# A gated cross-attention and channel-mix block: softmax denominators summed on ScalarE, queries stacked through DRAM, values loaded in two parts

## The chip, the cores and the metric

One core of one Trainium2 chip runs the whole program. The metric is device time in microseconds; three runs of the kernel before give a median of 3099.62 (3092.7 to 3100.64).

## What is computed

64 independent batches of 256 tokens with 512 features; 16 heads of 32 features. Cut to what matters, all in fp32:

```python
q = layernorm(x)                                   # [64, 256, 512]
qs, ks, vs = relu(heads(q)), relu(heads(ctx)), relu(heads(ctx))
att = softmax(einsum('bthf,byhf->bhty', qs, ks) / sqrt(32))
o = einsum('bhty,byhf->bhtf', att, vs)
x = x + tanh(g_xattn) * relu(o @ ffn_w.T + ffn_b)
n = layernorm(x); n_prev = n shifted by one token
xr, xk = mu_r * n + (1 - mu_r) * n_prev, mu_k * n + (1 - mu_k) * n_prev
x = x + tanh(g_ffn) * sigmoid(xr @ W_r) * (square(relu(xk @ W_k)) @ W_v)
```

## The kernel before

Matmul operands that need more precision than the fast matmul type gives are split into a high and a low part. A dense product is three matmuls (high x high, low x high, high x low; `product`, L944). For the scores, 96 rows hold the pieces instead: q as high, high, low and k as high, low, high, over 32 features each.

The work is a software pipeline over batches. An iteration `i` holds the attention of batch i, the projection and mixing of batch i - 1, the channel mix of batch i - 2 and the last sums of batch i - 3. The loop body is written twice, for the two values of `par`. Each engine has its own list of calls in `iteration`; those lists, written by hand, set the order of work. An engine executes its list strictly in order and waits on semaphores. On TensorE (the list from L1005) an iteration has 16 **slots**. Slot k begins with `shifted_scores(i, k)` (L911) and holds two dense parts (`dense`), six matmuls of 256 or three of 512 columns each, and the scores of the head seven further on.

The steps of attention in that order:

- `scores` (L899) computes query by key scores of one head into one of two PSUM banks, `s_bank`. `head_max` (L693, VectorE) takes each row's negative maximum, from which `turn_m` (L877), `copy_m` (L702) and the DMA `move_m` (L277) make row 96 of `q_st`. `scores` waits for `s_maxed` of the head two before.
- `shifted_scores` (L911) computes key by query scores with the maximum subtracted; `exponent` (L492, ScalarE) makes `probs` from them. The factor 1/sqrt(32) is the exponent's `scale`.
- `values` (L925) multiplies four heads' `probs` with `v_pos`. `denominators` (L937) multiplies the same `probs` with ones. `norm_o` (L712, L714, VectorE) takes the reciprocal of 128x256 denominators and multiplies.
- `write_o`, `read_o` (SP) carry the result through DRAM into `o_mv`. `o_high` (L499, ScalarE) and `o_low` (L362, GpSimd) split it, and `project` uses it.
- For q, `norm_1` (L663, VectorE) normalizes `x_ln`; `q_high` (L465, L466, ScalarE, two copies) and `q_low` (L669, VectorE) make `q_nat`. Eight `turn_q` (L868) per batch turn it, and eight `q_stack` (L473, ScalarE) copy it to `q_st`.
- `load_x1` (L451) and `load_v` (L457) are DMAs in ScalarE's queue. `load_x1` waits for the store of an earlier batch. `relu_v` (L684) is VectorE's.

All turns (of q, maxima and normalized x1) share one PSUM bank, `tp_bank`, and each waits for the copy that empties it:

```python
users = [copy_of(*t) for t in reversed(turns[:n])]
users += [copy_of(t[0], t[1] - 1, *t[2:]) for t in reversed(turns)]
```

Of the kernel before, what the change touches and what calls it, by code (L numbers as in the profile page):

```python
# [16 lines left out]
def flamingo_block(nc, x, ctx_in, ctx_t, g_xattn, g_ffn, w_t, bias, mu, out):  # L17
# [24 lines left out]
    SCALE = float(HD) ** -0.5  # L42
# [5 lines left out]
    with es:  # L48
# [10 lines left out]

        k_dram = nc.dram_tensor("k_dram", [2, CH, 2, HD, GR, T], F32, kind="Internal").ap()  # L60

# [4 lines left out]
        q_nat = sb("q_nat", [P, NU, HEADS, 3, HD], F32R)  # L66
# [6 lines left out]
        o_val = sb("o_val", [P, T])  # L73
        o_mv = sb("o_mv", [P, 2 * GR, T // GR])
# [45 lines left out]
        v_loaded = sem("v_loaded")  # L120
# [19 lines left out]
        q_stacked = sem("q_stacked")  # L140
# [11 lines left out]
        pv_ready = sem("pv_ready")  # L152
        rden_ready = sem("rden_ready")
        o_ready = sem("o_ready")
# [32 lines left out]
        out_ready = sem("out_ready")  # L187

# [30 lines left out]
        def _(sp):  # L219
# [13 lines left out]
            def load_x(b):  # L233
                if on(b):

                    after(sp, q_lo_ready, 2 * b)
                    after(sp, q_hi_ready, 2 * b)

# [32 lines left out]

            def move_m(b, c):
# [22 lines left out]

            def store(b, par):
                if on(b):
                    sp.wait_ge(out_ready, NU * (b + 1))
                    sp.dma_start(out[b].rearrange("(u p) d -> p u d", p=P), x1[:, par, :, :]).then_inc(stored, 16)

            def iteration(i, par):
                stack_k(i, 3, par)
                store(i - 3, 1 - par)
# [12 lines left out]
                stack_k(i + 1, 2, 1 - par)  # L316
                move_m(i + 1, 0)
                load_w(i)
                read_o(i, 0)
                write_o(i, 2)  # L320
# [13 lines left out]
        def _(pool):  # L334
# [15 lines left out]
            def rstd_2(b, u):  # L350
                if on(b):
# [3 lines left out]
                                            ALU.pow).then_inc(rstd2_ready, 1)  # L355

# [50 lines left out]
            def iteration(i, par):  # L407
                rstd_1(i + 1)
                ka_square(i - 2, 0)
                ka_square(i - 2, 1)  # L410
                o_low(i - 1, 1)
# [8 lines left out]
                xk_low(i - 1, 1)  # L420
                o_low(i, 0)
# [5 lines left out]
        def _(act):  # L427
# [25 lines left out]
            def load_v(b):  # L453
                if on(b):

                    after(act, pv_ready, CH * b)
                    act.dma_start(v_pos[:, :, :], ctx_in[b].rearrange("(v p) d -> p v d", p=P)).then_inc(v_loaded, 16)  # L457

            def q_high(b, u):
                if on(b):  # L460
                    act.wait_ge(x_normed, NU * b + u + 1)

                    after(act, q_turned, 2 * CH * b)
# [720 lines left out]
```

## Time and profile before

| what | value |
|---|---|
| median of three runs | 3099.62 us |
| the profiled execution | 3097.49 us, its span 3095.6 us |
| instructions | 70938 |
| TensorE's mean granted clock | 0.988 |
| DMA | 408.56 MB, mean 132 GB/s |

The page gives busy time by engine. Matmuls are pipelined, so TensorE's busy share says that something was in the array, not that it streamed at its peak. The chain of waits follows the last instruction back through whatever released each step, and "issue" in it is time for which the profile shows no cause. `PEld` is TensorE's weight load, `SPq` and `ACTq` are the sequencers of SyncE and ScalarE at work on DMAs.

### The profile page before, as it was taken

How to read it: one execution, taken by the hardware profiler on the slowest of the kernel's cores; microseconds unless marked ns; L12 is line 12 of the kernel's file. 1: busy time of each engine (PE TensorE's matmuls, PEld its weight loads, DVE VectorE, ACT ScalarE, POOL GpSimd, SP SyncE). 2: the span in 40 equal slices, each digit the busy share in tenths (PEclk: the TensorE clock that was granted, in tenths of full speed). 3: DMA queues.
4: the chain of work that ended last, by engine and by line, in shares of the span. 5: the costliest groups of instructions: out<-in, count | busy, mean ns of one | idle time of the engine just before them, and what ended most of it. 6: DMA issues, size and time to landing. Idle time of an engine off the chain costs nothing.

```text
span 3095.6 us, 70938 instructions
## 1 busy us (share of the span) xinstructions
PE 2882.7 (93%) x23168; PEld 2202.3 (71%) x23168; DVE 2326.9 (75%) x4111; ACT 1568.8 (51%) x2828; POOL 1049.3 (34%) x902
## 2 busy tenths in 40 slices
PE   3899999999999999999999999999999999999998
PEld 2677777777777777777777777777777777777776
DVE  5777777777777777777877777777777777778774
ACT  3445455455554555454555555554554545555542
POOL 0233333333332333333333333333333333333333
PEclk9999999999999999999999999999999999999999
DMA  4544435535435445445445354454454444454431
GB/s 163 147 125 132 143 110 149 149 108 151 140 115 149 135 124 146 127 131 144 125 135 147 107 150 137 118 152 129 125 149 127 131 143 125 140 146 130 132 107 40
DMA packets 387850, 408.56 MB, mean 132 GB/s; under 512 B 163553, under 2 KB 295649, under 8 KB 387810
## 3 DMA queue, kind: packets, MB, share of 16 engines
q1 hardware_dynamic: 352994, 340.92, 38.6%
q10 hardware_dynamic: 34816, 67.12, 6.7%
q8 instruction: 24, 0.39, 0.1%
q14 instruction: 16, 0.13, 0.0%
HBM read 272.64 MB, written 134.22 MB: 131 GB/s over the span
## 4 chain that ended last, share of the span: by engine, by line
PE 57%; DVE 15%; DMA 9%; issue 8%; SPq 7%; ACT 1%; ACTq 1%; DVEq 0%; POOL 0%; POOLq 0%
PE bank L944 28%; DMA out_dram<-x 8%; PE bank L925 7%; PE bank L911 6%; PE bank L899 5%; PE bank L937 4%; DVE m_nat L693 4%; DVE o_val L712 4%; SPq L270 3%; DVE st L647 2%; DVE k_raw L677 2%; PE bank L886 2%; PE bank L868 2%; SPq L256 2%; SPq L268 2%
## 5 line engine op out<-in xcount | busy, mean ns | idle before, releaser
L492 ACT ACTIVATE probs<-bank 128x512 f32<-128x512 f32 x1024 | 596.3, 593 | 481.4 <-PE bank L911 260.4
L693 DVE TENSOR_REDUCE m_nat<-bank 128x2 fp32r<-128x512 f32 x1024 | 688.4, 683 | 79.4 <-PE bank L899 78.7
L473 ACT ACTIVATE q_st<-bank 96x512 fp32r<-96x512 f32 x512 | 304.5, 595 | 717.2 <-PE bank L868 717.0
L911 PE MATMUL bank<-q_st,k_st 97*128 97x256 f32 x2048 | 451.3, 302 | 61.0 <-ACT probs L492 43.0
L712 DVE RECIPROCAL o_val<-bank 128x256 f32<-128x256 f32 x256 | 449.1, 1754 | 62.3 <-PE bank L937 54.5
L911 PEld LDWEIGHTS bank<-q_st,k_st 97*128 97x128 f32 x2048 | 341.7, 191 | 154.1 <-issue 56.4
L899 PE MATMUL bank<-k_st,q_st 96*128 96x256 f32 x2048 | 431.3, 293 | 7.6 <-DMA k_st<-k_dram 5.0
L899 PEld LDWEIGHTS bank<-k_st,q_st 96*128 96x128 f32 x2048 | 357.9, 192 | 59.6 <-issue 6.4
L395 POOL TENSOR_TENSOR xm<-xm 128x512 f32<-128x512 f32 x128 | 133.6, 1043 | 782.6 <-ACT xm L536 782.6
L925 PE MATMUL bank<-probs,v_pos 128*32 128x256 f32 x4096 | 282.0, 393 | 99.3 <-issue 98.6
L362 POOL TENSOR_TENSOR o_lo<-o_mv,o_hi 128x512 fp32r<-128x512 f32 x128 | 164.3, 1284 | 524.9 <-ACT o_hi L499 524.9
L702 DVE CAST m_t<-bank 4x256 fp32r<-4x256 f32 x256 | 105.0, 410 | 270.5 <-PE bank L877 270.4
L944 PE MATMUL bank<-xk_hi,w_hi 128*128 128x256 f32 x1024 | 298.4, 291 | 0.0
L944 PE MATMUL bank<-xk_lo,w_hi 128*128 128x256 f32 x1024 | 286.5, 280 | 0.0
L944 PE MATMUL bank<-xk_hi,w_lo 128*128 128x256 f32 x1024 | 286.3, 280 | 0.0
L937 PE MATMUL bank<-probs,ones_r 128*32 128x256 f32 x4096 | 284.4, 397 | 0.0
L925 PEld LDWEIGHTS bank<-probs,v_pos 128*32 128x32 f32 x4096 | 113.5, 110 | 222.6 <-issue 150.4
L868 PEld LDWEIGHTS bank<-ident_r,q_nat 128*96 128x96 f32 x2048 | 193.6, 127 | 71.3 <-issue 52.4
L868 PE MATMUL bank<-ident_r,q_nat 128*96 128x128 f32 x2048 | 219.7, 231 | 24.1 <-DVE q_nat L669 20.5
L380 POOL TENSOR_TENSOR xk_lo<-xm,xk_hi 128x512 fp32r<-128x512 f32 x128 | 164.4, 1285 | 215.1 <-ACT xk_hi L523 183.4
L354 POOL TENSOR_TENSOR rstd<-ve,mhalf 128x1 f32<-128x1 f32 x128 | 69.3, 542 | 446.2 <-DVE ve L730 446.2
L944 PE MATMUL bank<-w_hi,o_hi 128*128 128x512 f32 x512 | 209.4, 409 | 4.2 <-POOL o_lo L362 4.2
(90 smaller groups left out, 6128.1 us busy)
## 6 DMA issues: line engine op xcount, KB each, us to landing
k_st<-k_dram SPq DMA_DIRECT2D x256, 256.0 KB, 3.7
k_raw<-ctx_t_dram SPq DMA_DIRECT2D x256, 128.0 KB, 4.2
x_ln<-x_dram SPq DMA_DIRECT2D x256, 128.0 KB
k_dram<-k_high SPq DMA_DIRECT2D x64, 512.0 KB, 3.0
k_dram<-k_raw SPq DMA_DIRECT2D x64, 512.0 KB, 4.5
k_st<-k_dram SPq DMA_DIRECT2D x256, 128.0 KB, 3.6
v_pos<-ctx_dram ACTq DMA_DIRECT2D x64, 512.0 KB, 5.8
o_dram<-o_val SPq DMA_DIRECT2D x256, 128.0 KB, 1.7
```

Source lines behind the costliest of these rows:

```text
L362: nc.gpsimd.tensor_tensor(by_tile(o_lo, u), o_mv[:, :, :].rearrange("p g (k a) -> p k g a", k=KC), by_tile(o_hi, u).bitcast(F32), ALU.subt ...
L380: nc.gpsimd.tensor_tensor(xk_lo[:, part, :], xm[:, part, :], xk_hi[:, part, :].bitcast(F32), ALU.subtract).then_inc(xk_lo_ready, 1)
L473: nc.scalar.activation(q_st[0:QK, c, :, P * u:P * u + P], tp_bank[0:QK, :].rearrange("p (g t) -> p g t", g=GR), ACT.Copy).then_inc(q_stack ...
L492: nc.scalar.activation(probs[:, n // GR % 2, n % GR, :, :].rearrange("p v t -> p (v t)"), st_bank[n % 2][:, :], ACT.Exp, scale=SCALE).then ...
L693: nc.vector.tensor_reduce(m_nat[:, c % 2, :, n % GR:n % GR + 1], s_bank[n % 2][:, :].rearrange("p (u y) -> p u y", u=NU), AX_X, ALU.max, n ...
L712: nc.vector.reciprocal(o_val[:, :], pv_bank[:, T:2 * T]).then_inc(rden_ready, 1)
L868: mm = nc.tensor.transpose(tp_bank[0:QK, P * g:P * g + P].bitcast(F32R), q_nat[:, u, GR * c + g, :, :], ident_r[:, :])
L899: mm = nc.tensor.matmul(s_bank[n % 2][:, T * u:T * u + T], q_st[0:QK, c, g, P * u:P * u + P], k_st[0:QK, c, g, :], start=True, stop=True)
L911: mm = nc.tensor.matmul(st_bank[n % 2][:, T * v:T * v + T], k_st[0:ST, c, g, P * v:P * v + P], q_st[0:ST, c, g, :], start=True, stop=True)
L925: nc.tensor.matmul(pv_bank[HD * g:HD * g + HD, 0:T], v_pos[:, v, HD * h:HD * h + HD], probs[:, c % 2, g, v, :], start=(v == 0), stop=(v == ...
L937: mm = nc.tensor.matmul(pv_bank[HD * g:HD * g + HD, T:2 * T], ones_r[:, 0:HD].bitcast(F32), moving, start=(n == 0), stop=(n == len(sums) - 1))
L944: mm = nc.tensor.matmul(dst, lhs[a], rhs[c], start=first and n == 0, stop=last and n == 2)
```

## The change

- **Denominators.** `denominators` is gone. `sum_exp(b, n, par)` on ScalarE takes the exponents of one head's query by key scores in place in `s_bank`, with the head's negative maximum as bias, in two instructions of 128x256 (one per half of the queries); the accumulator output writes the sum to `den`. `scores` now waits for `s_summed` of the head two before. Per batch VectorE takes one reciprocal of 128x32 (`recip`), TensorE turns it (`turn_rden`), VectorE copies it (`copy_rden`). SP writes it to DRAM (`write_rden`) and reads it back in four DMAs, broadcast over 32 partitions (`read_rden`). GpSimd multiplies `o_mv` by it in place (`o_scale`), before `o_high`. `norm_o` becomes a plain copy (`copy_o`).
- **Scale.** The 1/sqrt(32) moves into the layer norm's variance, which is multiplied by 32, so that the maximum and both scores carry it.
- **Queries.** `norm_1` writes the normalized x with its features in another order to `q_low_t`. Two `turn_q` per batch turn it in fp32, four 128x128 transposes each. `q_high` takes one relu out of PSUM, `q_low` the rest. `write_q` and `stack_q` carry both parts through `q_dram` into `q_st`, in four and eight DMAs per batch. `q_stack` is gone.
- **Values.** Columns 0 to 383 of batch i + 1 are loaded in iteration i, behind `exponent(i, 14)`; columns 384 to 511 of batch i in iteration i. `relu_v` follows in two parts.
- **Order.** `norm_1` stands right behind `head_max(i, 7)`, and `load_x1` behind `exponent(i, 3)`.

```diff
+            def write_q(b, par):
+                if on(b):
+                    sp.wait_ge(q_hi_ready, NU * (b + 1))
+                    sp.wait_ge(q_lo_ready, NU * (b + 1))
+                    for u in range(NU):
+                        for half, tile in enumerate((x_ln[:, u, :].rearrange("p (c t) -> p c t", c=CH),
+                                                     q_low_t[:, u, :, :])):
+                            sp.dma_start(q_dram[par, :, half].rearrange("c f g t -> (f g) c t")[:, :, P * u:P * u + P],
+                                         tile).then_inc(q_written, 16)
+            def stack_q(b, c, par):
+                if on(b):
+                    sp.dma_start(q_st[0:HD, c, :, :].bitcast(F32), q_dram[par, c, 0]).then_inc(q_stacked[c], 16)
+                    sp.dma_start(q_st[HD:QK, c, :, :].bitcast(F32),
+                                 q_dram[par, c].rearrange("h f g t -> (h f) g t")).then_inc(q_stacked[c], 16)
...
+            def read_rden(b):
+                if on(b):
+                    sp.wait_ge(rden_written, 16 * (b + 1))
+                    for m in range(GR):
+                        sp.dma_start(rd_mv[HD * m:HD * m + HD, :, :],
+                                     rden_dram.rearrange("h (m r) -> m h r", m=GR)[m:m + 1].broadcast_to([HD, HEADS, T // GR])
+                                     ).then_inc(rd_moved, 16)
...
             def iteration(i, par):
                 stack_k(i, 3, par)
+                stack_q(i, 3, par)
                 store(i - 3, 1 - par)
...
                 stack_k(i + 1, 0, 1 - par)
+                write_q(i + 1, 1 - par)
                 move_m(i, 2)
+                queries_written(i + 1)
+                stack_q(i + 1, 0, 1 - par)
                 write_o(i, 0)
                 stack_k(i + 1, 1, 1 - par)
+                stack_q(i + 1, 1, 1 - par)
                 load_x(i + 2)
...
+            def o_scale(b, u):
+                if on(b):
+                    pool.wait_ge(rd_moved, 16 * GR * (b + 1))
+                    pool.wait_ge(o_moved, 16 * GR * (NU * b + u + 1))
+                    nc.gpsimd.tensor_tensor(o_mv[:, :, :], o_mv[:, :, :], rd_mv[:, 2 * GR * u:2 * GR * u + 2 * GR, :],
+                                            ALU.mult).then_inc(o_scaled, 1)
...
             def q_high(b, u):
                 if on(b):
+                    act.wait_ge(q_turned, NU * b + u + 1)
+                    nc.scalar.activation(x_ln[:, u, :].bitcast(F32R), tp_bank[:, :], ACT.Relu).then_inc(q_hi_ready, 1)
...
+            def sum_exp(b, n, par):
+                if on(b):
+                    act.wait_ge(s_maxed, HEADS * b + n + 1)
+                    for u in range(NU):
+                        scores = s_bank[n % 2][:, T * u:T * u + T]
+                        last = nc.scalar.activation(scores, scores, ACT.Exp,
+                                                    bias=m_nat[:, n // GR % 2, u, n % GR:n % GR + 1].bitcast(F32),
+                                                    accum_out=den[:, par, n, u:u + 1])
+                    last.then_inc(s_summed, 1)
...
             def scores(b, n):
...
-                        pe.wait_ge(q_stacked, 2 * CH * b + 2 * c + 2)
+                        pe.wait_ge(q_stacked[c], 32 * (b + 1))
                         pe.wait_ge(k_stacked[c], 32 * (b + 1))
-                    after(pe, s_maxed, HEADS * b + n - 1)
+                    after(pe, s_summed, HEADS * b + n - 1)
...
-                turns = [("q", i, 2, 1), ("m", i, 1, 0), ("q", i, 3, 0), ("q", i, 3, 1),
-                         ("m", i, 2, 0), ("q", i + 1, 0, 0), ("q", i + 1, 0, 1), ("q", i + 1, 1, 0),
-                         ("x", i - 1, 0, 0), ("m", i, 3, 0), ("x", i - 1, 0, 1), ("q", i + 1, 1, 1),
-                         ("m", i + 1, 0, 0), ("q", i + 1, 2, 0)]
+                turns = [("m", i, 1), ("q", i + 1, 0), ("q", i + 1, 1), ("m", i, 2),
+                         ("x", i - 1, 0), ("m", i, 3), ("x", i - 1, 1), ("rden", i, 0), ("m", i + 1, 0)]
```

Three places in the order of instructions matter below. First ScalarE around the exponent of slot 2 (`probs<-bank`). Before, from the load of x1 in front of it to the load of the values:

```order
L192 ISA
L451 ISA [waits stored]
L451 DMA x<-x_dram 128x2x512
L485 REGISTER_ALU
L492 ACTIVATE probs<-bank 128x512 [waits st_ready]
L533 ISA
L535 REGISTER_ALU [waits kt_ready]
L536 ACTIVATE xm<-bank 128x512 [waits xk_lo_ready]
L470 REGISTER_ALU
L473 ACTIVATE q_st<-bank 96x4x128 [waits st_ready,q_turned]
L457 ISA [waits pv_ready]
L457 DMA v_pos<-ctx_dram 128x2x512
```

After, from the same exponent to the values' load (L555 is `sum_exp`, L529 `q_high`, L601 `kt_relu`):

```order
L546 ACTIVATE probs<-bank 128x512 [waits st_ready]
L552 REGISTER_ALU
L555 ACTIVATE bank,den<-bank,m_nat 128x256 [waits s_maxed]
L555 ACTIVATE bank,den<-bank,m_nat 128x256
L528 ISA
L529 ACTIVATE x_ln<-bank 128x512 [waits q_turned]
L598 ISA
L600 REGISTER_ALU [waits kt_ready]
L601 ACTIVATE xm<-bank 128x512 [waits xk_lo_ready]
L208 ISA
L522 ISA [waits pv_ready]
L522 DMA v_pos<-ctx_dram 128x2x128
```

The load of x1 has left this place, the values' load is a quarter of its size, and the relu of q comes behind two summing exponents.

Second, TensorE at the second turn of q, at the end of slot 2, in the kernel after:

```order
L1030 MATMUL bank<-xk_hi,w_lo 128x256
L1030 MATMUL bank<-xk_lo,w_hi 128x256
L1030 MATMUL bank<-xk_hi,w_hi 128x256
L1030 MATMUL bank<-xk_hi,w_lo 128x256
L1030 MATMUL bank<-xk_lo,w_hi 128x256
L955 REGISTER_ALU
L958 MATMUL bank<-ident_r,q_low_t 128x128 [waits q_lo_ready,x_normed]
L958 MATMUL bank<-ident_r,q_low_t 128x128 x3
L208 REGISTER_ALU
L1009 MATMUL bank<-q_st,k_st 128x256 [waits exp_ready]
```

The four transposes wait for `q_lo_ready`, the low half of the first turn; the next shifted scores stand behind them.

Third, GpSimd at the start of an iteration. Before:

```order
L395 TENSOR_TENSOR xm<-xm 128x512 [waits kt_relued]
L393 REGISTER_ALU
L395 TENSOR_TENSOR xm<-xm 128x512 [waits kt_relued]
L359 ISA
L362 TENSOR_TENSOR o_lo<-o_mv,o_hi 128x4x128 [waits z_ready,o_hi_ready]
L388 TENSOR_TENSOR xr_lo<-xd,xr_hi 128x1024 [waits r_ready,xr_hi_ready,xr_ready]
```

After:

```order
L458 TENSOR_TENSOR xm<-xm 128x512 [waits kt_relued]
L456 REGISTER_ALU
L458 TENSOR_TENSOR xm<-xm 128x512 [waits kt_relued]
L415 ISA
L416 ISA [waits rd_moved]
L417 TENSOR_TENSOR o_mv<-o_mv,rd_mv 128x512 [waits o_moved]
L425 TENSOR_TENSOR o_lo<-o_mv,o_hi 128x4x128 [waits z_ready,o_hi_ready]
```

The scaling of `o_mv` stands between the second squaring (of what `kt_relu` gives) and the low part of o.

## Rows read from the trace of the kernel before

**Rows 1.** The page, part 1: busy us, share of the span, instructions.
```profile
PE 2882.7 (93%) x23168; PEld 2202.3 (71%) x23168; DVE 2326.9 (75%) x4111; ACT 1568.8 (51%) x2828; POOL 1049.3 (34%) x902
```

**Rows 2.** The chain that ended last, 1500 to 1600 us: start, length, what.
```profile
1503.72 0.38 ACTq L451
...
1509.52 1.17 issue
...
1517.79 0.24 PE bank L911 x2
1518.03 0.70 PE bank L944 x3
...
1524.55 1.00 PE bank L937 x16
1525.55 0.59 PE bank L886 x4
...
1528.94 0.25 PE bank L868 x4
...
1549.93 0.39 ACTq L451
...
1555.70 2.75 issue
...
1599.08 0.39 ACTq L451
```

**Rows 3.** Waits, whole run: who for whom: us in total, times, longest.
```profile
ACT probs L492 <- DMA out_dram<-x: 210.9, 60, 5.1
...
DVE v_pos L684 <- DMA v_pos<-ctx_dram: 133.5, 61, 3.3
...
PE bank L911 <- ACT probs L492: 43.0, 60, 2.3
```

**Rows 4.** Windows: stretch, length, busy by engine, TensorE's granted clock, DMA share, GB/s.
```profile
1551.00:1558.50 7.50, 4.67 (x25) 3.44 (x29) 2.14 (x4) 4.82 (x11) 2.08 (x2) 1.00 1.00 262
1558.50:1564.00 5.50, 5.50 (x46) 3.46 (x47) 3.64 (x5) 3.33 (x6) 3.90 (x2) 0.69 0.23 48
```

**Rows 5.** Timeline of ScalarE: start, length, instruction.
```profile
1552.92 1.08 ACT L492 ACTIVATE probs<-bank 128x512 f32<-128x512 f32 x2
```

**Rows 6.** Groups by form, 1500 to 1788 us, ScalarE: busy us, mean ns | idle before.
```profile
L492 ACT ACTIVATE probs<-bank 128x512 f32<-128x512 f32 x97 | 56.5, 593 | 48.3 <-DMA out_dram<-x 24.2 <-PE bank L911 23.2
...
L481 ACT ACTIVATE k_high<-k_raw 128x1024 fp32r<-128x1024 f32 x6 | 6.3, 1048 | 0.0
```

**Rows 7.** Timeline of VectorE around the start of an iteration.
```profile
1542.48 0.68 DVE L763 SCALAR_TENSOR_TENSOR th<-th,bank 128x512 f32<-128x512 f32 x1
1543.19 0.75 DVE L766 SCALAR_TENSOR_TENSOR x<-th,tgh,x 128x512 f32<-128x512 f32 x1
1543.86 0.41 DVE L702 CAST m_t<-bank 4x256 fp32r<-4x256 f32 x1
1544.47 1.76 DVE L712 RECIPROCAL o_val<-bank 128x256 f32<-128x256 f32 x1 [0.20 <-PE bank L937]
...
1546.60 1.66 DVE L755 SCALAR_TENSOR_TENSOR xd<-xd,mu_sb,xt 128x256 f32<-128x256 f32 x4
1548.18 0.68 DVE L693 TENSOR_REDUCE m_nat<-bank 128x2 fp32r<-128x512 f32 x1
1548.79 0.99 DVE L663 TENSOR_SCALAR x_ln<-x_ln,mv,rstd 128x512 f32<-128x512 f32 x2
1549.69 1.28 DVE L693 TENSOR_REDUCE m_nat<-bank 128x2 fp32r<-128x512 f32 x2
```

**Rows 8.** Groups by form, 1500 to 1788 us, GpSimd.
```profile
L362 POOL TENSOR_TENSOR o_lo<-o_mv,o_hi 128x512 fp32r<-128x512 f32 x12 | 15.4, 1283 | 44.6 <-ACT o_hi L499 44.6
L395 POOL TENSOR_TENSOR xm<-xm 128x512 f32<-128x512 f32 x12 | 12.5, 1042 | 74.6 <-ACT xm L536 74.6
```

**Rows 9.** The page, part 2: what the DMA moved.
```profile
DMA packets 387850, 408.56 MB, mean 132 GB/s; under 512 B 163553, under 2 KB 295649, under 8 KB 387810
```

More of the change, by code:

```diff
@@ L139, in flamingo_block @@
         q_turned = sem("q_turned")
-        q_stacked = sem("q_stacked")
+        q_written = sem("q_written")
+        q_stacked = [sem(f"q_stacked{c}") for c in range(CH)]
         v_ready = sem("v_ready")
@@ L410, in iteration @@
                 ka_square(i - 2, 1)
+                o_scale(i - 1, 1)
                 o_low(i - 1, 1)
@@ L420, in iteration @@
                 xk_low(i - 1, 1)
+                o_scale(i, 0)
                 o_low(i, 0)
@@ L924, in values @@
                             h = GR * c + g
-                            nc.tensor.matmul(pv_bank[HD * g:HD * g + HD, 0:T], v_pos[:, v, HD * h:HD * h + HD],
-                                             probs[:, c % 2, g, v, :], start=(v == 0), stop=(v == NU - 1))
-            def denominators(b, c):
-                if on(b):
-                    after(pe, o_ready, CH * b + c)
-                    sums = [[probs[:, c % 2, g, v, :] for g in range(GR)] for v in range(NU)]
-                    for n, per_head in enumerate(sums):
-                        for g, moving in enumerate(per_head):
-                            mm = nc.tensor.matmul(pv_bank[HD * g:HD * g + HD, T:2 * T], ones_r[:, 0:HD].bitcast(F32),
-                                                  moving, start=(n == 0), stop=(n == len(sums) - 1))
+                            mm = nc.tensor.matmul(pv_bank[HD * g:HD * g + HD, 0:T], v_pos[:, v, HD * h:HD * h + HD],
+                                                  probs[:, c % 2, g, v, :], start=(v == 0), stop=(v == NU - 1))
                     mm.then_inc(pv_ready, 1)
@@ L1052, in iteration @@
                 values(i - 1, 3)
-                turn(1)
-                denominators(i - 1, 3)
+                turn(0)
                 dense(0, 2)
@@ L1057, in iteration @@
                 dense(0, 3)
-                turn(2)
+                turn(1)
                 shifted_scores(i, 2)
@@ L1080, in iteration @@
                 values(i, 0)
-                turn(4)
-                denominators(i, 0)
+                turn(3)
                 shifted_scores(i, 6)
-                turn(5)
                 dense(3, 0)
@@ L1092, in iteration @@
                 scores(i, 14)
-                turn(6)
                 dense(3, 3)
@@ L1098, in iteration @@
                 scores(i, 15)
-                turn(7)
                 dense(4, 1)
@@ L1104, in iteration @@
                 values(i, 1)
-                turn(8)
+                turn(4)
                 scores(i + 1, 0)
                 dense(4, 3)
-                turn(9)
+                turn(5)
                 shifted_scores(i, 10)
                 dense(5, 0)
-                denominators(i, 1)
-                turn(10)
+                turn(6)
                 scores(i + 1, 1)
@@ L1120, in iteration @@
                 dense(5, 3)
-                turn(11)
+                turn(7)
                 shifted_scores(i, 12)
@@ L1130, in iteration @@
                 values(i, 2)
-                turn(12)
+                turn(8)
                 scores(i + 1, 4)
@@ L1137, in iteration @@
                 scores(i + 1, 5)
-                denominators(i, 2)
-                turn(13)
                 dense(7, 1)
```

189 lines of the change are left out of this document (115 added, 74 removed).

## The prediction

> **What bounds the kernel now.** The busy line comes first: TensorE is busy 93% of the span, VectorE 75%, ScalarE 51% [rows 1]. So TensorE sets the pace, and the questions are how much matmul time an iteration holds and what makes TensorE wait. The profiled execution took 3097.5 us (span 3095.6), 0.07% under the median of 3099.6. A difference under about 0.3% could not be told from no change here.
>
> The chain of waits gives the period. Its load of x1 comes at 1503.72, 1549.93 and 1599.08 us [rows 2], so two iterations take 95.36 us, and one 47.68. The same rows show two kinds of loss: "issue" stalls of 1.17 and 2.75 us in front of the matmuls with the values. The waits by pair tell why [rows 3]. VectorE waits 133.5 us in 61 times for the values' DMA. That DMA stands in ScalarE's queue behind the load of x1, which waits for the store of an earlier batch (210.9 us in 60 times). TensorE's next shifted scores then wait for the late exponent, 43.0 us in 60 times, 0.7 each. In the stretch before the 2.75 us stall the DMA engines are full (share 1.00, 262 GB/s), and behind it TensorE's granted clock is 0.69 for 5.5 us, a mix of its two levels, 1.2 and 2.4 GHz [rows 4]. The shorter stall of the neighbouring iteration leaves no such mark.
>
> **The matmuls removed and added.** Per batch four groups of denominators go, 1.00 us each, and eight turns of q at 0.25 [rows 2]: 6.0 us. Two q turns of full width come in; the turn of xn has their form (0.59), so 1.18. The turn of the 32 columns of reciprocals is a single transpose; between nothing and a whole 0.25 turn I take 0.15. Net: 4.65 us less.
>
> **The stalls removed.** Three quarters of the values are now loaded a whole iteration ahead, the last quarter a few slots ahead of its use, and the load of x1 moves behind `exponent(i, 3)`. The values' stall goes, (1.17 + 2.75) / 2 = 1.96 us, and the 0.7 for the exponent. The slow clock cost 5.5 x (1 - 0.69) = 1.7 us in every second iteration, 0.85 per iteration. Together 3.5 us. What is late next is treated below. The **floor** is thus 47.68 - 4.65 - 3.5 = 39.5 us.
>
> **ScalarE.** It was busy 1568.8 / 64 = 24.5 us per batch. Eight stackings of q and two of the four copies into high parts go; two exponents back to back take 1.08 us and one 0.59 [rows 5, 6], so the step is 0.49; about 4.9 us go and 19.6 stay. Added are 32 exponents of 256 columns that also sum. Nothing in the trace sums on ScalarE, so both bounds: at the low end, the step of 0.49 less 256 columns at (1048 - 593) / 512 = 0.89 ns [rows 6], that is 0.26 us, if bias and sum are free; at the high end 0.9, if the sum needs a second pass through the engine's fixed part, a whole 512-wide record (0.59) and 0.3 more. I take 0.5, nearest to the 512-wide step. That gives 19.6 + 16 = 35.6 us: ScalarE becomes as full as VectorE was, but not the bound. The Trainium skill (ScalarE: Activation LUTs, What ACT_TABLE_LOAD costs) puts a bias column at about 93 ns on top and names no price for the sum; by it an exponent would be about 0.35 us and ScalarE at 30.8. No row here shows it.
>
> **VectorE.** Four reciprocals of 1.76 us and their products go, and a copy of about 0.41 (the CAST's row, also out of PSUM) comes in each time [rows 7]. The reciprocal of 32 columns, the copy of the turned reciprocals and the split relu add under 1 us. VectorE falls from 36 to about 30 us per batch.
>
> **New wait one, at the second q turn.** The two q turns share one PSUM bank with all the others, and `turn(2)` waits for `q_low(i+1, 0)`. Count from the scores of head 7. VectorE: max 0.6, norm_1 0.9 (moved up here), finish 1.4, copies 0.4 + 0.4, mix_r 1.6, max of head 8 0.7 [rows 7], taken from start to start, 6.0 together. ScalarE: two summing exponents 1.0, then `q_high` 0.6, since `q_high` is queued behind them. VectorE's `q_low` 0.7. With four hand-overs of 0.1 it is 8.7 us. TensorE has in the meantime five dense parts of 0.70, four pairs of score matmuls of 0.24, the values 1.0, a q turn 0.59 and a turn of maxima of 0.15 [rows 2]: 6.2. Stall: 2.5 us. Queued behind it are the shifted scores and all dense work.
>
> **New wait two, at `o_scale`.** It stands on GpSimd behind `ka_square(i-2, 1)`, which waits for `kt_relu(i-2, 1)`; and ScalarE, right after that relu, waits for `o_scale` in `o_high(i-1, 1)`. From the shifted scores of slot 4: 0.24, exponent 0.6, two sums 1.0, relu 0.6, square 1.04, scale 1.1, `o_high` 0.6, `o_low` 1.28 [rows 8], seven hand-overs 0.7: 7.1 us until project's second half may start. TensorE's own work until there is five pairs of score matmuls, four dense parts, the values, a turn of maxima and two bias matmuls of a quarter us: 5.6. Stall: 1.5 us.
>
> Of these 4.0 us I charge 2.8: the floor was reached by subtraction and still holds small gaps of the old order at the same places, and a wait ahead shortens the next. **Sum:** 39.5 + 2.8 = 42.3 us per iteration, 5.4 less; 3097.5 - 64 x 5.4 = 2752 us. Ramp and tail are left as they are.
>
> **DMA and SP.** The run moves 408.56 MB [rows 9]. Per batch come 1.05 MB of q written, 1.57 MB of q stacked and 0.52 MB of reciprocals read in pieces of 256 B: 3.15 MB, 202 MB in all, 610 MB. At 262 GB/s [rows 4] that is 2330 us of 2752, 85%. I charge nothing, because each stack is needed some three slots after it may be issued. If that cover is gone, a row of maxima (`move_m(i, 2)`), issued behind 1 MB of q writes, arrives late: 1 MB at that rate is 4 us, against eight us of slack.
>
> **Rivals.**
> - **All waits hidden.** If q's low half and `o_scale` fit under the matmuls, the floor stands: 3097.5 - 64 x 8.2 = 2573. For it: the exponents run two heads ahead. Against: both chains above are longer than their cover. Chance 0.12.
> - **Late data or dearer sums.** At 0.75 us a sum ScalarE has 19.6 + 24 = 43.6 us and takes over; with 0.9 of waiting, 44.5 us. A late row of maxima costs 2 us on 42.3 and gives about the same. 3097.5 - 64 x 3.2 = 2893. Chance 0.21.
> - **The clock stays low after the stall.** The 2.75 us stall left 0.69, the 1.17 us one did not. The forecast's first stall lies between them; if it costs 1.7 us in each iteration, 44.0 us, 2862. The Trainium skill (TensorE: Matmul & The Clock Gate, What's actually happening) says that idleness throttles and activity releases it. The trace agrees: 1.00 fell to 0.69 only behind the longer stall. Chance 0.12.
> - **Slower: ScalarE becomes the bound above the old period.** Scores of head n + 2 may not overwrite a bank before head n's sum is done, so a dear sum stops everything. It decides from (47.7 - 19.6) / 32 = 0.88 us per sum; at 0.95, one iteration is 50 us, 3097.5 + 64 x 2.3 = 3245. For it: no row prices the sum. Against: a whole 512-wide exponent out of PSUM takes only 0.59. Chance 0.05.
>
> **How the numbers follow.** The forecast has 0.50, 2752 us. The range 2590 to 2930 takes in most of it, of the dearer sums and of the low clock; outside are the floor case and the slower one. Faster by over 0.3%: 0.94; within 0.3%: 0.01; slower: 0.05.
>
> **What would show it.** Right: no L937 group, period near 42.3 us, no VectorE wait on the values' DMA, ScalarE's busy time near 2280 us, TensorE waits at the second q turn for VectorE's `q_low`, ScalarE waits for GpSimd before `o_high`. Wrong: a sum's step far from 0.5 us; waits on q_st or k_st DMAs; granted clock well under 0.95; TensorE without gaps.

## The result, and the profile after

The changed kernel takes **3310.32 us** (median of four runs, 3304.26 to 3318.21) against 3100.13 of the kernel before: a ratio of 1.0681, 95% interval 1.0647 to 1.0715. The forecast was 2752, with a range to 2930.

The page's part 1, with the clock and the DMA from part 2, of the kernel after. It answers to [rows 1] and [rows 9]:

```profile
PE 2716.8 (82%) x17600; PEld 2137.0 (65%) x17600; DVE 2057.9 (62%) x4047; ACT 2165.0 (65%) x6284; POOL 1188.9 (36%) x1030
...
PEclk9698999999998999998989999999889999999999
...
DMA packets 711432, 610.94 MB, mean 184 GB/s; under 512 B 313057, under 2 KB 611041, under 8 KB 711394
```

TensorE is busy 82% of the span where it had 93%, and VectorE 62% where it had 75%. ScalarE rose from 51% to 65% with its sums, and GpSimd from 34% to 36%. So no engine took over the bound; they wait for one another. TensorE's mean granted clock is 0.917 instead of 0.988.

The page's part 5, the new sums on ScalarE (`sum_exp`, L555): count | busy us, mean ns | idle before:

```profile
L555 ACT ACTIVATE bank<-bank,m_nat 128x256 f32<-128x256 f32 x2048 | 928.0, 458 | 189.9 <-DVE m_nat L772 183.3
...
L555 ACT ACTIVATION_READ_ACCUMULATOR bank<-bank,m_nat 128x1 f32 x2048 | 444.9, 217 | 0.0
```

Each sum is two records that overlap in part. Timeline of ScalarE after:

```profile
1540.06 0.45 ACT L555 ACTIVATE bank<-bank,m_nat 128x256 f32<-128x256 f32 x1 [1.12 <-DVE m_nat L772]
1540.44 0.19 ACT L555 ACTIVATION_READ_ACCUMULATOR bank<-bank,m_nat 128x1 f32 x1
1540.53 0.44 ACT L555 ACTIVATE bank<-bank,m_nat 128x256 f32<-128x256 f32 x1
1540.89 0.20 ACT L555 ACTIVATION_READ_ACCUMULATOR bank<-bank,m_nat 128x1 f32 x1
1540.98 0.60 ACT L616 ACTIVATE th<-bank 128x512 f32<-128x512 f32 x1
```

From one start to the next it is 0.47 and 0.45 us. That term held.

Waits of the kernel after, from 300 to 2900 us (us in total, times, longest). Against [rows 3], no wait for the values' DMA is left:

```profile
POOL o_mv L417 <- DMA rd_mv<-rden_dram: 338.7, 52, 7.8
ACT o_hi L564 <- POOL o_mv L417: 331.5, 104, 4.4
DVE q_low_t L740 <- POOL rstd L403: 266.7, 52, 5.6
...
PE bank L997 <- ACT bank L555: 146.2, 107, 3.0
...
PE bank L958 <- DVE m_t L781: 106.7, 52, 2.4
...
PEld bank L1009 <- DMA q_st<-m_t: 74.7, 52, 3.9
PE bank L1009 <- DMA q_st<-m_t: 54.3, 45, 3.5
```

TensorE's largest wait is for ScalarE's sums (L555), which must empty a bank before the scores two heads later are written: 146.2 us, 2.8 per iteration. TensorE's timeline over one iteration shows the rows in front of which it stood:

```profile
1545.20 0.50 PE L1009 MATMUL bank<-q_st,k_st 97*128 97x256 f32 x2 [2.06 <-DMA q_st<-m_t]
...
1562.57 0.51 PE L997 MATMUL bank<-k_st,q_st 96*128 96x256 f32 x2 [2.18 <-ACT bank L555]
...
1566.21 1.12 PE L958 MATMUL bank<-ident_r,q_low_t 128*128 128x128 f32 x4 [2.43 <-DVE m_t L781]
...
1571.08 0.63 PE L958 MATMUL bank<-ident_r,q_low_t 128*128 128x128 f32 x4 [0.34 <-DVE q_low_t L748]
...
1580.42 0.47 PE L1030 MATMUL bank<-w_hi,o_hi 128*128 128x512 f32 x1 [1.05 <-POOL o_lo L425]
...
1591.61 0.65 PE L984 MATMUL bank<-ident_r,xn 128*128 128x128 f32 x4 [0.77 <-DVE xn L824]
```

The first stall is for a row of maxima (`move_m`), a DMA of 4 KB. The second (for a sum) and the third (the first q turn, for the bank that `copy_m` empties) have one root. Four timelines of the kernel after show it, first SyncE's queue:

```profile
1545.11 0.30 SPq L333 DMA_DIRECT2D rden_dram<-rd_t  x1
1551.61 0.66 SPq L311 DMA_DIRECT2D q_st<-m_t  x1
1552.39 1.84 SPq L326 DMA_DIRECT2D o_mv<-o_dram  x4
1554.34 2.00 SPq L340 DMA_DIRECT2D rd_mv<-rden_dram  x4
```

The reciprocals are written at 1545.11 but read back only at 1554.34, because `move_m(i + 1, 0)` and `read_o` stand between. Then GpSimd, VectorE and ScalarE:

```profile
1559.18 1.28 POOL L417 TENSOR_TENSOR o_mv<-o_mv,rd_mv 128x512 f32<-128x512 f32 x1 [7.51 <-DMA rd_mv<-rden_dram]
1561.19 1.26 POOL L425 TENSOR_TENSOR o_lo<-o_mv,o_hi 128x512 fp32r<-128x512 f32 x1 [0.74 <-ACT o_hi L564]
1562.41 0.70 POOL L403 TENSOR_TENSOR rstd<-ve,mhalf 128x2 f32<-128x2 f32 x1
```

```profile
1563.24 1.29 DVE L740 TENSOR_SCALAR q_low_t<-x_ln,mv,rstd 128x512 f32<-128x512 f32 x2 [4.72 <-POOL rstd L403]
```

```profile
1560.49 0.63 ACT L564 ACTIVATE o_hi<-o_mv 128x512 fp32r<-128x512 f32 x1 [3.58 <-POOL o_mv L417]
```

GpSimd stands 7.51 us for the reciprocals (`o_scale(i, 0)`). Behind that instruction in its list is `rstd_1(i + 1)`, the reciprocal root of the layer norm, and VectorE's `norm_1`, moved up by the change, stands 4.72 us for it with its whole list behind it. ScalarE waits 3.58 us in `o_high`, with its sums behind it. So the bank of the scores is emptied late by ScalarE and the bank of the turns by VectorE, and TensorE stops twice. The clock follows, in stretches of the same iteration (columns as in [rows 4]):

```profile
1560.00:1565.00 5.00, 1.60 (x12) 1.19 (x10) 1.76 (x3) 3.43 (x11) 2.37 (x3) 0.89 1.02 289
1565.00:1570.00 5.00, 3.79 (x18) 3.79 (x19) 4.70 (x11) 1.89 (x6) 0.00 (x0) 0.50 0.37 139
```

With TensorE busy for 1.60 of 5 us, the granted clock was 0.50, the level of 1.2 GHz, in the 5 us that follow.

**Periods.** In the kernel after, the write of the reciprocals starts 47 times between 338.3 and 2652.4 us: 50.31 us a period. The load of x1 in the kernel before gives 47.05 in the same way (51 starts, 326.8 to 2679.4); the 47.68 of the forecast came from two iterations only. All periods below are measured so, over 300 to 2700 us.

### The profile page after: what moved, and what is told of

Same layout as the page of the kernel before. It is cut to its first block and busy times, and to the rows that moved or that the text cites. A ratio compares the mean times of both kernels' runs of the same rounds, so it can differ in the third digit from the quotient of the medians.

```text
span 3311.6 us, 63464 instructions
## 1 busy us (share of the span) xinstructions
PE 2716.8 (82%) x17600; PEld 2137.0 (65%) x17600; DVE 2057.9 (62%) x4047; ACT 2165.0 (65%) x6284; POOL 1188.9 (36%) x1030
## 5 line engine op out<-in xcount | busy, mean ns | idle before, releaser
L555 ACT ACTIVATE bank<-bank,m_nat 128x256 f32<-128x256 f32 x2048 | 928.0, 458 | 189.9 <-DVE m_nat L772 183.3
L555 ACT ACTIVATION_READ_ACCUMULATOR bank<-bank,m_nat 128x1 f32 x2048 | 444.9, 217 | 0.0
L564 ACT ACTIVATE o_hi<-o_mv 128x512 fp32r<-128x512 f32 x128 | 80.7, 631 | 409.9 <-POOL o_mv L417 409.9
L417 POOL TENSOR_TENSOR o_mv<-o_mv,rd_mv 128x512 f32<-128x512 f32 x128 | 163.8, 1280 | 470.5 <-DMA rd_mv<-rden_dram 460.6
L1030 PE MATMUL bank<-xk_hi,w_lo 128*128 128x256 f32 x1024 | 325.7, 318 | 0.0
L1030 PE MATMUL bank<-xk_lo,w_hi 128*128 128x256 f32 x1024 | 324.9, 317 | 0.0
L740 DVE TENSOR_SCALAR q_low_t<-x_ln,mv,rstd 128x512 f32<-128x512 f32 x128 | 83.7, 740 | 319.5 <-POOL rstd L403 319.5
L958 PE MATMUL bank<-ident_r,q_low_t 128*128 128x128 f32 x512 | 121.4, 382 | 184.3 <-DVE m_t L781 124.3
L1030 PEld LDWEIGHTS bank<-xk_hi,w_hi 128*128 128x128 f32 x1024 | 234.3, 229 | 0.5 <-issue 0.4
L1030 PEld LDWEIGHTS bank<-xk_hi,w_lo 128*128 128x128 f32 x1024 | 234.2, 229 | 0.1
```

Of the source, the lines that this page charges most:

```text
L417: nc.gpsimd.tensor_tensor(o_mv[:, :, :], o_mv[:, :, :], rd_mv[:, 2 * GR * u:2 * GR * u + 2 * GR, :], ALU.mult).then_inc(o_scaled, 1)
L555: last = nc.scalar.activation(scores, scores, ACT.Exp, bias=m_nat[:, n // GR % 2, u, n % GR:n % GR + 1].bitcast(F32), accum_out=den[:, par ...
L958: mm = nc.tensor.transpose(tp_bank[:, P * c:P * c + P], q_low_t[:, u, c, :], ident_r[:, :].bitcast(F32))
L1030: mm = nc.tensor.matmul(dst, lhs[a], rhs[c], start=first and n == 0, stop=last and n == 2)
```

## The experiments

The edits are small moves in the lists of calls, or one part of the change alone. Times are compared with the kernel before, run beside them.

### The values alone

The kernel before with the values' part (two loads, `relu_v` in two parts, `load_x1` behind `exponent(i, 3)`):

```diff
-                load_v(i)
+                load_v(i, 1)
-                load_x1(i - 1, 1 - par)
...
                 exponent(i, 3)
+                load_x1(i - 1, 1 - par)
...
                 exponent(i, 14)
+                load_v(i + 1, 0)
```

> The kernel before with the values loaded in two parts and the load of x1 behind exponent(i, 3), nothing else of the change. By the prediction's term for the stalls removed (3.5 us per iteration): 3097 - 64 x 3.5 = 2873 us. Rival: TensorE only waits elsewhere (turns of q in their shared bank), gain under 1 us per iteration, over 3035 us.

Measured: 2916.92 us, **0.937** (0.9339 to 0.9402), clock 0.997, period 44.07. That is 2.98 us an iteration under 47.05, of 3.5 in the forecast. TensorE is busy 97% of the span, and its list of waits from 300 to 2700 us holds this one alone:

```profile
PE bank L950 <- POOL o_lo L364: 14.0, 37, 1.0
```

So this part is sound. The rest of the change costs 393 us on top of it (3310.32 against 2916.92), more than the whole loss of 210.

### Queries and values, without the denominators' part

The changed kernel with `denominators` and `norm_o` as before, without `sum_exp`, `recip`, `o_scale` and the reciprocals' way through DRAM.

> The change without its denominators: queries through DRAM and values in two parts as in the kernel after, denominators, reciprocals and their product as in the kernel before. If the denominators' path (sums on ScalarE, reciprocals through DRAM and GpSimd) makes the kernel slow: under 2950 us, at or under the 2917 of the values alone, since eight q turns of 0.25 us become two of 0.59. If the bulk of the queries' DMA does, through rows of maxima that stand behind it in SP's queue: over 3150 us.

Measured: 3256.66 us, 1.0527 (1.0493 to 1.056), clock 0.948. Its waits from 300 to 2900 us have one dominant pair on TensorE:

```profile
PE bank L939 <- DVE q_low_t L728: 221.9, 53, 4.3
...
PE bank L990 <- DMA q_st<-m_t: 14.8, 24, 1.1
```

This is the "new wait one" of the forecast, at the second q turn: 4.2 us an iteration instead of 2.5. In the iteration read, VectorE's block in front also holds a reciprocal of 1.74 us here, and `mix_r` took 2.45 us instead of 1.66; that they make up the difference is argued, not tried. The time lies in the range that was set for late rows of maxima, but these account for 14.8 us only: neither of the two explanations put on record fits. The queries' part brings 340 us over the values alone; the denominators' part adds only some 50 more, with other stalls.

### Three orders

First, the reciprocal roots ahead of the scaling on GpSimd:

```diff
-                rstd_1(i + 1)
                 ka_square(i - 2, 0)
...
                 xk_low(i - 1, 1)
+                rstd_1(i + 2)
                 o_scale(i, 0)
```

> The kernel after, with GpSimd's rstd_1 of the next batch moved one iteration up, ahead of o_scale(i, 0). Theory A (the late reciprocals reach TensorE through GpSimd's queue: o_scale, o_low, rstd_1, then norm_1 at the head of VectorE's list): VectorE's wait of 5.1 us per iteration for rstd_1 and TensorE's 2.4 us wait at the first q turn go with the slow clock behind it, period 51.4 to about 47 us, 3030 us in all; TensorE's wait for the sum of head 5 behind o_high stays. Theory B (DMA traffic of 611 MB makes rows of maxima and stacks late) and theory C (the summing exponents are too dear): unchanged within 1%, 3310 us.

Measured: 3189.69 us, 1.0268 (1.0221 to 1.0315), clock 0.955, period 48.05.

Second, the reciprocals read right behind their write on SyncE:

```diff
                 write_rden(i)
+                read_rden(i)
                 move_m(i + 1, 0)
                 load_w(i)
                 read_o(i, 0)
-                read_rden(i)
```

> The kernel after, with read_rden issued right behind write_rden on SP, ahead of the row of maxima and of read_o. Theory A: the reciprocals land some 6 us earlier, GpSimd's wait for rd_mv (6.5 us per iteration) shrinks under 2, and both stalls at the start of an iteration go (2.2 and 2.4 us and the slow clock): about 46 us per iteration, 2960 us. Theory B: the same bytes flow, so 3310 us within 1%. Theory C: unchanged.

Measured: 3204.25 us, 1.0279 (1.0237 to 1.032), clock 0.936, period 48.75. Each order takes 1.6 to 2.3 us off the 50.31: the path of the reciprocals is a cause. Both fell short of the 3030 and 2960 expected.

TensorE's waits from 300 to 2700 us show that the late reciprocals reach it by two ways, one per order. With the roots first, its wait for `copy_m` at the first turn, 97.7 us in the kernel after, is gone, and the one for the sums stays (144.2 against 134.9). With the read first, the wait for the sums falls to 47.7 us and the one for `copy_m` stays (120.6). GpSimd then stands 204.7 us for the next thing in line, the outputs (`read_o`).

Third, both together, with the row of maxima ahead of the load of x:

```diff
-                load_x(i + 2)
                 move_m(i, 3)
+                load_x(i + 2)
```

> Both reorderings and move_m(i, 3) ahead of load_x(i + 2) on SP; no work changed. Theory A with a late row of maxima as its second part: no GpSimd wait for rd_mv reaches TensorE, and the 2.06 us wait of the shifted scores for q_st<-m_t goes too: 42 to 44 us per iteration, 2740 to 2870 us. Theory B: the row of maxima stays late, little gained over the second run. Theory C: not under 3200 us.

Measured: 3224.15 us, 1.0355 (1.032 to 1.039), no better than either alone and far from the 2740 to 2870 expected. The two orders without the third:

> The third run without its exchange of move_m(i, 3) and load_x(i + 2): rstd_1 early on GpSimd and read_rden early on SP. If x's load, now in front of the reciprocals in the same queue, spoiled the third run: about 3120 us, under both single reorderings. If the two reorderings hand the same wait to each other: about 3200 us as each alone.

Measured: 3248.3 us, 1.0487 (1.0447 to 1.0526). Two edits that help singly are worse together, so they uncover something. In the run with two orders the waits for `copy_m` and the sums are down to 6.8 and 43.2 us, but two others have grown, from 24.0 us at the second turn and 50.2 us for the row of maxima in the kernel after:

```profile
PE bank L1009 <- DMA q_st<-m_t: 148.7, 60, 4.9
PE bank L958 <- DVE q_low_t L748: 107.2, 48, 2.3
```

The second is the forecast's "new wait one", at its forecast size (2.2 us each), which the longer stall ahead of it had covered. For the first, the run with three orders shows SyncE's timeline:

```profile
1545.94 0.54 SPq L254 DMA_DIRECT2D x_ln<-x_dram  x1
...
1549.60 0.42 SPq L333 DMA_DIRECT2D rden_dram<-rd_t  x1
1555.97 1.91 SPq L340 DMA_DIRECT2D rd_mv<-rden_dram  x4
1558.01 0.67 SPq L311 DMA_DIRECT2D q_st<-m_t  x1
```

Its list of DMAs by issue (KB each, median us from issue to landing), the same row of the run with two orders, and the stretch of that wait in the run with three say:

```profile
rden_dram<-rd_t SPq DMA_DIRECT2D x49, 16.0 KB, 6.7
```

```profile
rden_dram<-rd_t SPq DMA_DIRECT2D x48, 16.0 KB, 3.7
```

```profile
1549.60:1556.00 6.40, 6.40 (x47) 4.77 (x46) 4.04 (x11) 5.80 (x18) 3.25 (x3) 1.00 0.74 188
```

A write of 16 KB takes 6.7 us to land (3.7 with two orders, 2.0 in the kernel after), SyncE's queue stands for it, and the next row of maxima leaves late; yet the DMA engines are busy only 0.74 on the mean. The load of x, 512 KB, ended its issue 3.1 us before, with five other transfers between. In the iterations read it began 6.0 us ahead of the write here, since the third order moved it back, and 9.8 us or more ahead in the other two kernels. What is full is not the sixteen engines together.

### Without the division

```diff
-                write_rden(i)
...
-                read_rden(i)
...
-                o_scale(i, 0)
```

> The kernel after without write_rden, read_rden and o_scale: the output stays undivided by the denominators, which are still summed, inverted, turned and copied. If the reciprocals' way (DMA and GpSimd) is the cause: 42 us per iteration, 2740 us. If DMA traffic of the queries and late rows of maxima are: 48 us or more, over 3100 us, with the wait of the shifted scores for q_st<-m_t unchanged at 2 to 3 us per iteration.

The output of this kernel stays undivided. Measured: 3336.87 us, 1.0768 (1.0724 to 1.0812). With the reciprocals' path gone altogether the kernel is no faster than the changed one (1.0681). Other waits took their place, as with the two orders:

```profile
PE bank L1004 <- DMA q_st<-m_t: 230.0, 85, 5.4
```

The row of maxima issued behind the load of x came late, 230.0 us in 300 to 2700 us against 50.2 in the kernel after, and the wait at the second turn rose from 24.0 to 108.9 us. So the reciprocals were not the only cause. This run was not repeated with the load of x that follows below.

### The stacks of q from ScalarE's queue

Both orders, and `stack_q` issued by ScalarE, behind `exponent` 8, 9, 11 and 15:

> The run above with the eight stack_q DMAs per batch issued from ScalarE's queue instead of SP's; the bytes are the same. If the small transfers (rows of maxima, reciprocals, o) are late because they stand behind bulk in SP's own queue: the wait for q_st<-m_t falls under 0.5 us per iteration and the time under 3000 us. If the 16 DMA engines are simply too full: within 1% of the run above.

Measured: 3499.09 us, 1.1303 (1.1266 to 1.134), the slowest. Its waits from 300 to 2900 us have a new one on TensorE, for the stacks themselves:

```profile
PE bank L999 <- DMA q_st<-q_dram: 204.8, 48, 4.8
```

ScalarE's list now holds the wait for q's writes, and its exponents and sums stand behind it; TensorE waits 184.6 us for sums. The row of maxima, though, did come earlier: TensorE's wait for it fell from 148.7 to 36.3 us in 300 to 2700 us. So a freer SyncE helps that row too, but did not pay for the rest, and the run does not say where the DMAs collide.

### The load of x over sixteen rows a transfer

```diff
-                    for m in range(GR):
-                        part = slice(P // 2 * (m % 2), P // 2 * (m % 2) + P // 2)
-                        sp.dma_start(x_ln[part, m // 2, :],
-                                     x[b].rearrange("(a k m) d -> m k a d", k=KC, m=GR)[m]).then_inc(x_loaded, 16)
+                    for k in range(KC):
+                        for p in range(2):
+                            part = slice(P // 2 * p + 16 * k, P // 2 * p + 16 * k + 16)
+                            sp.dma_start(x_ln[part, :, :],
+                                         x[b].rearrange("(a k u p) d -> k p a u d", k=KC, u=NU, p=2)[k, p]
+                                         ).then_inc(x_loaded, 16)
```

> The changed kernel with one edit: x is loaded in eight transfers of 64 KB, each of 16 rows of the tile, in place of four of 128 KB whose outermost run has only four steps; same bytes, same order on SP. Theory A (a short transfer issued behind the load of x waits for a few of the sixteen DMA engines that the load occupies, while the mean share is below one): the wait of the shifted scores for the row of maxima (55.2 us in 46 of the waits, and 76.3 in 54 on the weight load, 2.06 us in the iteration read) falls to under a quarter, and the time falls by 50 to 120 us, to 3190 to 3260. Rival B (all sixteen are simply full at that place): four more issues on SP, no shorter wait, 3300 to 3340. In both the waits at the turns of the queries stay.

Measured: 3243.84 us, 1.0457 (1.0425 to 1.0488), period 49.33. TensorE's wait for the row of maxima, 50.2 us from 300 to 2700 us in the kernel after, does not occur in its list at all, nor does that of the weight load. With the two orders on top:

> The same load of x together with the two orders that helped singly (the reciprocal roots of norm_1 ahead of the scaling on GpSimd, the reciprocals of the denominators read right behind their write). Theory A: what kept the two orders from adding up (3248 for both, 3190 and 3204 for each alone) was the short write of the reciprocals and the rows of maxima behind the load of x; with it spread both add, 3050 to 3130, and the wait of the shifted scores for the row of maxima is under 20 us in the whole run. Rival B: 3200 to 3260 as without it.

Measured: **3018.72 us, 0.9735** (0.9707 to 0.9762), below the range I gave and faster than the kernel before. The same edit that took 1.0 us from the period alone turned 3248 into 3019. Its DMAs and waits:

```profile
rden_dram<-rd_t SPq DMA_DIRECT2D x53, 16.0 KB, 1.7
```

```profile
PE bank L960 <- DVE q_low_t L750: 117.6, 53, 2.3
...
PE bank L1011 <- DMA q_st<-m_t: 9.3, 16, 1.5
```

Against the same two orders without the spread, the write of 16 KB lands in 1.7 us instead of 3.7 (6.7 with three orders), and TensorE's wait for the row of maxima is 9.3 us instead of 148.7. With the spread the three edits add up: 0.98 (spread), 2.26 (roots) and 1.56 (read) are 4.80 us, and together they give 50.31 - 45.55 = 4.76.

The Trainium skill (DMA: Bandwidth & Descriptors, Why a DMA increments its semaphore by 16 and not by 1) says that a transfer runs on the largest number of engines up to 16 that divides the slowest dimension of both its sides, and on the lowest-numbered ones. By it the four-step load of x runs on four. The runs agree as far as they can show it: a transfer was held up at a mean share of 0.74, and no longer with sixteen steps. An estimate from [rows 4]: 262 GB/s over sixteen engines is 16.4 each, so 512 KB on four takes 8 us, on sixteen 2; behind the four-step load the write landed 5 us later with three orders, and 2 us later with two. The trace does not name the engines of a transfer, so their number is inferred from the cure. The edit also halves each transfer (eight of 64 KB for four of 128 KB); no run changes the number of steps and leaves the size, so smaller transfers alone are a rival that stands.

### A later second turn, and the outputs written first

```diff
                 dense(1, 1)
-                turn(2)
...
                 dense(1, 3)
+                turn(2)
```

on top of the spread and the two orders, with its `q_high` and `q_low` moved behind it, and `o_scale(i - 1, 1)` ahead of the second squaring on GpSimd. The two moves were not run apart.

> The kernel of the run above with the second turn of the queries moved from behind dense(1, 1) to behind dense(1, 3), some 2.5 us of TensorE later, its two copies on ScalarE and VectorE moved behind it, and the scaling of the older half put first on GpSimd. Theory C (what is left is the chain first turn, copy of the low half on VectorE, second turn in the same bank): the wait there, 1 to 4 us an iteration in every version so far, falls to under 0.7 us, the period to 44 to 46 us, the clock to over 0.96: 2880 to 3000. Rival D (any place is as bad, since VectorE's list between is as long): within 1% of the run above.

Measured: 2992.1 us, 0.9652 (0.9614 to 0.9691), period 45.13, clock 0.966. The stall at the turn is gone (0.8 us in 300 to 2700 us), as expected, but the time stands at the slow end of its range, since a stall of 2.48 us had formed at the projection. GpSimd and TensorE in that run:

```profile
1505.43 1.29 POOL L419 TENSOR_TENSOR o_mv<-o_mv,rd_mv 128x512 f32<-128x512 f32 x1 [4.86 <-DMA o_mv<-o_dram]
```

```profile
1509.08 0.47 PE L1032 MATMUL bank<-w_hi,o_hi 128*128 128x512 f32 x1 [2.48 <-POOL o_lo L427]
```

So one more order, on SyncE, with the later turn and without it:

```diff
-                store(i - 3, 1 - par)
-                move_m(i, 1)
                 write_o(i - 1, 3)
+                move_m(i, 1)
+                store(i - 3, 1 - par)
```

> The kernel with the later turn (2992, 0.965 of before) with one more edit: on SP the last quarter of the outputs of the batch before is written ahead of the row of maxima and of the store of 512 KB, in place of behind them. In the run of the later turn that write left SP at 1496.83, 1.6 us after its copy on VectorE ended, landed at 1501.0, and the scaling on GpSimd began at 1505.4; TensorE then stood 2.48 us for the low part of the outputs. Theory E (the new chain is this one: write, read back, scaling, halves): the stall falls by 1.5 to 2.5 us an iteration, to 2860 to 2920. Rival F (the DMA engines are full there and the order changes nothing, or the row of maxima becomes late instead): 2970 to 3000.

> The same edit without the later turn (on the kernel of 3019 us, 0.9735). Theory E: there the second turn still stalls 2.2 us and the outputs only 1.07, so 0.3 to 1 us an iteration, 2955 to 3000; if the stall at the turn only grows by what the outputs give back, 3010 to 3030.

Measured: with the later turn **2882.37 us, 0.9324** (0.9292 to 0.9355), period 43.22, clock 0.988; without it 2994.26 us, 0.9683 (0.9651 to 0.9714). Against the run with the spread and two orders (0.9735) the write alone gives half a per cent, the turn alone 0.42 us, both together 2.33: two chains in parallel, and only the longer one is seen. This is the lowest time of the study, and it is the change with most of its waits mended. But its interval overlaps that of the values alone (0.9339 to 0.9402), and its period is only 0.85 us shorter (43.22 against 44.07): queries and denominators together, mended, are worth little beyond the values' part. Its page, and its largest waits on TensorE:

```profile
PE 2584.7 (90%) x17600; PEld 1986.6 (69%) x17600; DVE 2043.2 (71%) x4047; ACT 2157.6 (75%) x6284; POOL 1202.5 (42%) x1030
```

```profile
PE bank L1011 <- DMA q_st<-m_t: 77.1, 89, 3.5
PE bank L999 <- ACT bank L557: 50.9, 108, 1.3
PE bank L1032 <- POOL o_lo L427: 36.0, 46, 1.7
```

### The mended queries without the denominators' part

Queries and values as above, with x spread, the roots earlier, the outputs written first and the second turn later.

> The queries' part and the values' part without the new denominators (3257, 1.053 of before by itself; the denominators and the division as in the kernel before), now with the mends of the best kernel so far: x in eight transfers, the reciprocal roots earlier on GpSimd, the last write of the outputs first on SP, the second turn later. It splits the gain of the mended kernel (2882, 0.932) between the parts. Theory G (the 4.65 us of matmuls that the change removes are really saved, most of them by the turns and the denominators, and the waits stood before them): without ScalarE's sums TensorE keeps the 64 short matmuls of the denominators, so 2900 to 2960, between the mended kernel and the values alone or a little above. Rival H (VectorE's block around norm_o holds the second turn also here): 3000 to 3150.

Measured: 3022.52 us, 0.972 (0.9689 to 0.9751), period 45.65: above the values alone, in the rival's range but not by its mechanism. The turn waits only 28.0 us in all; the larger wait is for the maxima of VectorE, which is busy 79% here:

```profile
PE bank L980 <- DVE m_nat L754: 76.9, 52, 1.5
```

So the queries' part without the denominators' does not pay, even mended. With the denominators' part, which takes four reciprocals off VectorE, the same mends gave 0.9324; that the reciprocals make that difference is argued from this wait, not tried.

### The spread load in the kernel with the values alone

> The kernel before with the values loaded in two parts (0.937 of before by itself) and x loaded in eight transfers over sixteen rows each. The rows of maxima follow the load of x there too, but the chain of waits named no row of maxima in the kernel before, so little is to be had: theory A 2890 to 2925, 0 to 0.9% under the values alone; if the load of x held a later transfer up there too, 2850 to 2890.

Measured: 2910.87 us, 0.9387 (0.9361 to 0.9412), no difference from the values alone (0.937). The four-step load is harmless there. That fits a kernel in which TensorE waits for no transfer behind it: of its waits from 300 to 2700 us, in either run, the only one is for the low part of o.

## Why the prediction was wrong

- **Stalls removed, 3.5 us.** Right in kind, 2.98 measured. Of it 0.9 is less busy time at the same matmuls (2280.7 of 2400 us at 47.05 is 44.7 an iteration, 2386.0 at 44.07 is 43.8), the 0.85 of the slow clock.
- **Matmuls, 4.65 us.** The mended kernel is busy 2212.4 of 2400 us, 39.8 an iteration, 4.0 under the values alone, at a clock of 0.988 against 0.997. Nearly right.
- **A sum of 0.5 us on ScalarE.** Right: 0.46 by step, and ScalarE busy 2165.0 us against the 2280 given. VectorE is at 2057.9 us, 32.2 per batch where about 30 was said. The slower rival, ScalarE as the bound, did not happen.
- **New wait one, 2.5 us.** Right in place and cause, but not seen in the changed kernel: there the second turn waits 0.5 us for `q_low` (24.0 us in 48 times), because the first turn had stood 2.0 us (97.7) just ahead of it for VectorE. It is 4.2 in the run with queries and values, and 2.2 with both orders, with the spread and without.
- **New wait two, `o_scale`: the step that failed.** Its working priced the instructions around `o_scale(i - 1, 1)` and gave it 1.5 us; that wait, at project's second half, came to 1.1 (54.7 us in 52 times). It left out `o_scale(i, 0)`, which waits for `read_rden` behind `move_m(i + 1, 0)` and `read_o` on SyncE, and what is queued behind it: `rstd_1` on GpSimd, for which `norm_1` blocks VectorE. Charged 0, it costs 3.8 us: 2.26 + 1.56 for the orders singly, and 49.33 - 45.55 = 3.78 for both on top of the spread.
- **"DMA and SP: I charge nothing": the second failure.** The slack of eight us was set against 1 MB at the rate of all engines, 4 us. The transfer that mattered was not 1 MB of q but the load of x, at a mean share under one. A late row of maxima stood among the rivals at 2 us, and nothing was charged for it in the sum. It is 1.0 us in the changed kernel, and it hid what the two orders were worth (3248 against 3019). The text had named waits on the DMAs of q_st and a clock well under 0.95 as what would prove it wrong, and both came (0.917).
- **A wait without a term: the bank of the scores.** `scores` waits for ScalarE's sum of the head two before. The forecast used this only for its slower rival, a dear sum; the sums were as cheap as forecast, and TensorE still waits for them, 2.8 us an iteration in the changed kernel and 1.3 with the spread and both orders (68.2 us).
- **The sum.** The changed kernel is 50.31 - 43.22 = 7.1 us above the mended one. TensorE's busy time is 2008.1 of 2400 us, 42.1 an iteration, 2.3 of it more than in the mended kernel for the same matmuls: that goes with the clock, 0.917 against 0.988. The other 4.8 is idleness. The low clock was a rival with its own chance; it came on top of the stalls, which the rivals had priced one at a time. Against the forecast of 42.3 the changed kernel is 8.0 us over: 3.8 for the reciprocals' way, 1.0 for the load of x, 2.3 for the later turn and the outputs first, and 0.9 that stay.
- **The 2.8 us charged for waits** were too few even with the two failed steps mended. With the spread and both orders the period is 45.55 and TensorE busy 40.1 of it (2114.6 of 2400 us), so it idles 5.4: 2.2 at the second turn, 1.3 for sums, 1.0 at the projection, 0.6 at the turn of normalized x1, the rest in small ones. The mended kernel idles 3.4 us, near the 2.8, but that is luck: the wait at the second turn is gone from it, and the largest is for rows of maxima.

What stays open: why the mended kernel still waits for its rows of maxima (77.1 us in 89 times), and whether the steps or the size of the load of x held the others up.

## What to carry to other kernels

When an instruction gains a wait, list what is behind it on its own engine, and then what each other engine has queued behind that. A small DMA is priced by its queue and by the shape of the transfers ahead of it, not by its bytes against the mean rate. When two edits help singly and hurt together, look for the third thing they uncover before undoing either: here the layout of one load stood between 1.0487 and 0.9735. And compare the mended whole with its best part alone: here it was hardly ahead of it.

## What was not expected of the hardware

- A transfer of 16 KB needed 6.7 us from issue to landing at a mean DMA share of 0.74 with the load of x begun 6.0 us ahead of it, and 3.7 in the order with it begun 9.8 us or more ahead. In that same order it needed 1.7 once the load was laid out in sixteen steps instead of four (eight issues instead of four cost nothing visible in the kernel with the values alone, 0.9387 against 0.937).
- An ACTIVATE with an accumulator output is followed by a record of its own, ACTIVATION_READ_ACCUMULATOR, mean 217 ns for 128x1. It overlaps the ACTIVATE's end and the next one's start, so the step is 0.46 us for 458 + 217 ns of records.
- Behind a stretch of 5 us in which TensorE was busy for 1.60 us, the granted clock was 0.50 for the next 5.
